# Seams of a two-layer transformer kernel: waits by bank, last value products, row copies and transposes are put elsewhere in the order

## The reference, cut to what matters

```
x = x + conv0(ln(x)); x = x + moe0(ln(x))     # layer 0
x = x + conv1(ln(x)); x = x + moe1(ln(x))     # layer 1
conv0: 12 heads of 32, all 1024 keys, relative position terms added to the scores,
       softmax, times values, output projection 384x384 with bias
conv1: 12 query heads, 4 key/value heads, a 7x7 window of keys, softmax, values, projection
moe  : logits = x @ Wr + b; the top 2 of 8 experts per token, softmax of the two;
       layer 0 routes only; layer 1 adds a shared expert of width 768
```

## Time and profile before

| What | Value |
|---|---|
| Median of three runs | 1117.99 us (1117.44 to 1119.78) |
| Profiled execution: time | 1120.67 us |
| Profiled execution: span of the instructions | 1119.1 us |
| PE busy | 1005.0 us, 90% of the span |
| DVE, ACT, POOL busy | 519.5, 322.8, 390.0 us |
| Mean granted clock of PE, share of full | 0.966 |

### The profile page before, as it was taken

How to read it: one execution, slowest core, us unless ns; L and a number is a source line. 1 busy time by engine, 2 the same in 40 slices (tenths; PEclk the granted TensorE clock), 3 DMA queues, 4 the chain that set the end, 5 groups by cost and what they waited for, 6 DMA issues and landing times.

```text
span 1119.1 us, 13486 instructions
## 1 busy us (share of the span) xinstructions
PE 1005.0 (90%) x4429; PEld 585.0 (52%) x4430; DVE 519.5 (46%) x910; ACT 322.8 (29%) x482; POOL 390.0 (35%) x333
## 2 busy tenths in 40 slices
PE   6999999999992499999588889899999999999998
PEld 3755555555441266665436655477444554455554
DVE  4555687788573055545446676671111111111114
ACT  3514545554621012222324545151111111111100
POOL 5514676677744201000533667353000000000004
PEclk9999999999996699999789999999999999999999
DMA  8699308000058235521326200613444434410005
GB/s 298 151 291 276 85 1 188 1 1 1 1 175 323 98 133 180 195 68 38 110 69 158 58 1 1 239 43 113 148 155 155 155 131 175 157 42 29 15 29 162
DMA packets 47177, 130.07 MB, mean 116 GB/s; under 512 B 7121, under 2 KB 26073, under 8 KB 46872
## 3 DMA queue, kind: packets, MB, share of 16 engines
q1 hardware_dynamic: 32360, 65.05, 19.7%
q0 software_dynamic: 14768, 64.37, 16.3%
HBM read 87.78 MB, written 30.61 MB: 106 GB/s over the span
## 4 chain that ended last, share of the span: by engine, by line
PE 72%; DVE 9%; issue 8%; DMA 4%; ACT 4%; POOL 1%; another core or an unknown queue 1%; SPq 0%; POOLq 0%; DVEq 0%; ACTq 0%
PE PS L1798 22%; PE PS L1819 11%; PE PS L1595 6%; PE PS L1513 5%; PE PS L1649 5%; PE PS L1771 4%; DMA Wd<-in_Wd_r 4%; DVE nmax_part L1239 3%; PE PS L1630 3%; PE PS L1735 3%; PE PS L1845 3%; PE PS L1632 2%; DVE exp_acc L1271 2%; PE PS L1573 2%; PE PS L1807 2%
## 5 line engine op out<-in xcount | busy, mean ns | idle before, releaser
L1798 PE MATMUL PS<-Wgu,xbT 128*128 x690 | 285.2, 555 | 9.2 <-DMA Wd<-in_Wd_r 5.5
L1798 PEld LDWEIGHTS PS<-Wgu,xbT 128*128 128x128 f32 x690 | 127.7, 191 | 127.3 <-issue 114.8
L1046 ACT ACTIVATE expS<-PS 128x1024 f32<-128x1024 f32 (+3 forms) x156 | 135.6, 878 | 119.2 <-PE PS L1632 117.6
L1819 PE MATMUL PS<-Wd,hidT 128*128 x414 | 143.0, 491 | 1.5 <-DVE hidT L1407 0.8
L843 POOL TENSOR_TENSOR exp_acc<-exp_acc,expS 128x512 f32<-128x512 f32 (+1 forms) x65 | 124.6, 1917 | 47.6 <-ACT expS L1046 46.8
L1239 DVE TENSOR_REDUCE nmax_part<-PS 128x1 f32<-128x512 f32 x160 | 103.7, 685 | 45.9 <-PE PS L1595 45.1
L1630 PE MATMUL PS<-QA,KS 128*128 128x512 f32 (+3 forms) x312 | 115.1, 375 | 9.8 <-ACT QB L1024 9.5
L1595 PE MATMUL PS<-KS,QA 128*128 128x512 f32 (+2 forms) x288 | 108.7, 423 | 13.2 <-DVE nmax L1239 5.2
L1632 PE MATMUL PS<-QB,KS 128*128 128x512 f32 (+3 forms) x312 | 110.7, 361 | 0.0
L1819 PEld LDWEIGHTS PS<-Wd,hidT 128*128 128x128 f32 x414 | 78.7, 191 | 57.7 <-issue 14.3
L947 POOL DMA_INDIRECT got<-block_rows_out,row_i x32 | 31.8, 993 | 209.1 <-DMA block_rows_out<-yb 199.9
(11 more groups left out here) (174 smaller groups left out, 1245.5 us busy)
## 6 DMA issues: line engine op xcount, KB each, us to landing
Wgu<-in_Wgu POOLq DMA_DIRECT2D x8, 1152.0 KB, 6.2
Wgu<-in_Wg_r POOLq DMA_DIRECT2D x8, 1152.0 KB, 6.2
Wgu<-in_Wu_r POOLq DMA_DIRECT2D x8, 1152.0 KB, 8.4
Wd<-in_Wd_r POOLq DMA_DIRECT2D x8, 1152.0 KB, 10.8
xb<-block_rows_in SPq DMA_DIRECT2D x46, 192.0 KB, 2.4
block_rows_out<-yb SPq DMA_DIRECT2D x46, 192.0 KB, 1.9
part_rows<-parts SPq DMA_DIRECT2D x2, 3072.0 KB, 17.4
Wd<-in_Wd POOLq DMA_DIRECT2D x8, 576.0 KB, 7.2
```

Source lines behind the costliest of these rows:

```text
L1046: act.activation(exp_tile(layer, c, unit)[:, pair, :].rearrange("p (b n) -> p b n", b=2)[:, :, lo:hi], PS[:, 2 * pair:2 * pair + 2, lo:hi] ...
L1798: last = pe.matmul(PS[:, 3 * par + lo // BANK, 0:n], xbT[:, par, kc, :], Wgu[layer][:, bass.ds(s, 1), kc, lo:lo + n], start=kc == 0, stop= ...
L1819: last = pe.matmul(PS[:, 7, 0:C], hidT[layer][:, par, i, :], Wd[layer][:, bass.ds(s, 1), i, :], start=i == 0, stop=i == m.IC - 1)
```

## The change: what it does

1. **Maxima wait by bank.** PE no longer waits for all jobs before the first piece. In layer 1 each of the first three pieces waits for the jobs in its own two banks; in layer 0, whose last jobs lie in banks 6 and 7, the pieces don't wait for jobs, and the first value product does.
2. **Last value products behind the rows.** In layer 0 one value product, in layer 1 two, move from between the pieces to behind `maxima_rows`; ACT copies them behind the first row copies.
3. **Row copies split within pairs.** In layer 1 ACT copied the rows of heads 0 and 1 and DVE those of 2 and 3. Now ACT copies 0 and 2, DVE 1 and 3, and ACT's second one stands behind the exponential of the unit's second pair.
4. **The last unit but one of layer 1** is no longer added up by POOL; PE sums it directly in `totals`, as it did already with the last.
5. **Transposes among projections.** The transposes of the first four tiles run before the last two projections, in both layers, and the first half's router product before the second half's transposes. ACT takes the second root after the copies of the first half.

Nothing that is computed changes, and no transfer is added.

The core of the diff:

```diff
-            if hb == 2 * BLOCKS - 1 and v == PER_HALF1 - 1:
+            if hb == 2 * BLOCKS - 1 and v >= PER_HALF1 - 2:
                 return []
...
+        VALUES_AHEAD = [NT - 1, NT - 2]
...
                 root(0)
-                if n % 2:
-                    root(1)
                 for kc in range(KC):
                     copy(0, kc)
-                if n % 2 == 0:
-                    root(1)
+                root(1)
                 copy(1, 0)
...
-                    if layer and pair:
-                        return
                     rows = 1 if layer == 0 else D
-                    for g in (2 * pair, 2 * pair + 1):
+                    for g in (2 * pair, 2 * pair + 1)[:2 - layer]:
...
-                for t in range(NT):
+                def copy_values(t):
...
+                for t in range(VALUES_AHEAD[layer]):
+                    copy_values(t)
...
                 copy_rows(0, 0, 0)
                 copy_rows(0, 0, 1)
+                for t in range(VALUES_AHEAD[layer], NT):
+                    copy_values(t)
...
-                    for g in range(2, G):
-                        last = dve.tensor_copy(QB[1][c % 2][D:2 * D, g, hb % HALF * BANK:(hb % HALF + 1) * BANK],
-                                               PS[D * g:D * g + D, 4, :])
-                    last.then_inc(nmax_dve, 1)
+                    for g in range(1, G, 2):
+                        dve.tensor_copy(QB[1][c % 2][D:2 * D, g, hb % HALF * BANK:(hb % HALF + 1) * BANK],
+                                        PS[D * g:D * g + D, 4, :]).then_inc(nmax_dve, 1)
...
-                for n in range(njobs - 8, njobs):
-                    evacuated(pe, layer, n)
...
+                    if t == 0:
+                        evacuated(pe, layer, 1 if layer else njobs - 1)
...
                     if hb % BLOCKS == 0:
+                        if layer and i < 3:
+                            evacuated(pe, layer, 2 * i + 3)
...
                     if u % (U[layer] // 2) == 0:
-                        if layer == 0:
-                            pe.wait_ge(nmax_act, 2 * (HALF * c + half) + pair + 1)
-                        elif pair == 0:
-                            pe.wait_ge(nmax_act, 2 * BLOCKS + HALF * c + half + 1)
-                        else:
-                            pe.wait_ge(nmax_dve, HALF * c + half + 1)
+                        pe.wait_ge(nmax_act, 2 * (BLOCKS * layer + HALF * c + half) + pair + 1)
+                        if layer:
+                            pe.wait_ge(nmax_dve, 2 * (HALF * c + half) + pair + 1)
...
-                    if end:
-                        lo, hi = units(layer)[U[layer] - 1][2:]
+                    for u in (range(U[layer] - 1 - layer, U[layer]) if end else ()):
+                        lo, hi = units(layer)[u][2:]
...
                     max_piece(first_block, i)
-                    if i % 2 == 1:
+                    if i % 2 == 1 and i // 2 < VALUES_AHEAD[layer]:
                         values(i // 2)
                 maxima_rows(first_block)
+                for t in range(VALUES_AHEAD[layer], NT):
+                    values(t)
...
                     last.then_inc(proj_psum, 1)
+                    if t == NT - 3:
+                        transposes(2 * layer + 1, 0)
...
-                transposes(2 * layer + 1)
+                router(layer, 0)
+                transposes(2 * layer + 1, 1)
+                router(layer, 1)
```

More of the change, by code:

```diff
@@ new lines, in transposes, with transposed @@
+            def transposes(n, half):
+                if n % 2:
+                    pe.wait_ge(proj_dve, NT * (n // 2) + 3 * (half + 1))
+                for kc in range(KC):
+                    for t in range(4 * half, 4 * half + 4):
+                        pe.wait_ge(xn_ready, NT * n + t + 1)
+                        last = pe.transpose(PS[:, 3 * half + kc, (t % 4) * P:(t % 4 + 1) * P], Xn[:, t, kc * P:(kc + 1) * P], ident[:, :])
+                    last.then_inc(xT_psum, 1)
+            def transposed(n, half):
+                pe.wait_ge(xT_act, 4 * n + 3 + half)
+                if half:
+                    pe.wait_ge(xT_dve, 2 * (n + 1))
@@ L1552, in _, with router @@
+            def router(layer, half):
+                transposed(2 * layer + 1, half)
+                pe.wait_ge(const_in, 16 * 4)
+                pe.wait_ge(proj_dve, NT * layer + 7 + half)
+                for kc in range(KC):
+                    last = pe.matmul(PS[0:E, 6 + half, :], router_w[:, layer, kc, :], XnT[:, kc, half * BANK:(half + 1) * BANK],
+                                     start=kc == 0, stop=kc == KC - 1)
+                last.then_inc(logits_psum, 1)
             for layer in range(2):
```

36 lines of the change are left out of this document (9 added, 27 removed).

## The result

The changed kernel takes 1107.1 us, the median of six runs (1104.3 to 1111.6), against 1117.6 us for the kernel before in the same six rounds (1112.1 to 1119.8): ratio 0.9923, 95% interval 0.9894 to 0.9952. A second set on another chip gave 1109.5 against 1116.6, ratio 0.9920 (0.989 to 0.995). By the two ratios 8.6 and 8.9 us are gone, about 8.8 (the medians of the first set are 10.5 apart); the forecast of 1110 had 8.0 us off the median shown before. One run of the experiments, of the kernel with part 3 alone, took 1499.53 us at a mean granted clock of 0.65 and counts in no ratio. The profiled execution of the changed kernel took 1107.34 us, with a span of 1105.8 us and a mean granted clock of 0.972. PE is busy for 1004.1 us of it, as before.

The account below looks back on a forecast made before the run. PE's waits at four seams, three idle stretches costing again by half clock, bound it. Terms 4.0 + 1.4 + 0.3 + 3.1 + 1.3 = 10.1; with clock parts halved, 8.2 off 1117.99: forecast 1110, range 1105.5 to 1114.

Parts of the forecast that it names:

- layer 0's seam: Start of layer 0's attention, PE's last job to the scores: 4.0 us gained, middle of 3.2 and 4.8.
- The steps on waits: At PE's seams: which wait ends last once the named one is gone, and the gain left by it.
- rival 3: Both layers' attention starts: transfers end last, taking away 1.7 + 1.35 and 1.1 us; 1114 us, chance 0.07.
- rival 1: Layer 0's router: its shortening counts there too, another 1.3 us; 1108.5 us, chance 0.08.
- rival 4: Layer 0's loop of 48 units: another rhythm, 0.33 us more wait per unit; 1125.8 us, chance 0.03.
- the price of half clock: Start of layer 0's attention: first two value-product passes 3.30 us, last 1.95, so 1.35 us lost.
- The start: Layer 0's attention: first value product starts at 65.4 instead of 67.12, 1.7 us gained.
- The clock parts: Gains from slowed stretches avoided in layer 0's attention start and layer 1's end: 1.35 + 0.8 + 1.7 = 3.9 us.
- a pair of terms: Layer 1's totals and projections, 3.1 us gained, and its router up to the shared expert, 1.3 us.
- two steps of part 4: Layer 1's totals: without clock 2.29 - 0.7 = 1.6, rounded to 1.4 us; clock gain counted half for the median.
- Rival 2: Whole kernel: clock gains are none, before lacking slowed stretches or the changed kernel getting its own; 1111.8 us, chance 0.20.
- six terms: Gains by seam: layer 0's attention 4.0; layer 1's 1.4, 0.3, 3.1 and 1.3; layer 0's router nothing.

Follow-up runs that it names:

- part 3 alone: Only the row copies split within pairs, on the kernel before: ratio 0.9990 (0.997 to 1.0011).
- parts 3, 4 and 5 alone: Three kernels, each the kernel before with just one of these parts: ratios 0.9990, 0.9971 and 0.9989.
- part 1 alone: Only the maxima's waits by bank, value products all still between the pieces, on the kernel before: 1114.62 us, ratio 0.9978.

## Why the prediction was right

Each seam without half clock and with it, in us, from the profiles named above:

| Seam | Without the part | With the part | Gain, like clock | Forecast |
|---|---|---|---|---|
| Layer 0: last job to first weighted product | 34.0, worked out below; 35.0 to 36.6 with half clock | 32.54; 34.2 with | 1.5 | 4.0, of it 1.8 without clock |
| Layer 1: last job to first scores | 13.09 | 11.48 | 1.6 | 1.4 |
| Layer 1: second to sixth rows | 68.79 | 68.61 | 0.2 | 0.3 |
| Layer 1: last rows to projections | 16.97; 17.2 to 18.3 with | 15.06 | 1.9 | 3.1, of it 1.4 without clock |
| Layer 1: projections to logits' transposes | 28.30 | 27.07 | 1.2 | 1.3 |
| Layer 0: projections to xb | 64.6 to 65.4 | 64.6 to 65.3 | 0 | 0 |

No profile of the old order is unfilled and at full clock over all of layer 0's seam. The 34.0 are 25.1 us to the rows (parts 3, 4 and 5 alone) and 8.9 from there on (part 1 alone). The kernel before with its idle time filled has 33.74: its first piece starts 0.10 us behind DVE's last low part instead of 0.35.

**The parts one by one.** By ratio parts 1 and 2 give 5.8 us, part 3 1.1, part 4 3.2 and part 5 1.2: 11.3 together, and 8.8 for all five. Each interval is about 2.2 us to either side, so the runs can't tell whether the parts add up. The seams say that part 3's 0.6 us is covered by part 2.

**The steps on waits held.** The waits that the forecast named are last: DVE's low part and not a transfer releases the value product (rival 3 falls), the reductions take the table load's place, PE itself is last in front of layer 1's scores, and in layer 0 POOL hides the router's gain (rival 1 falls). The loop of layer 0, from the first weighted product to the projections, takes 212.3 to 212.6 us in each of the fourteen profiles (rival 4 falls).

**The mis-sized term is layer 0's seam.** (The two rows that the forecast compared for the price of half clock, 3.30 and 1.95 us, are one value product of six passes each.) Its 4.0 us are exact for this pair of executions (36.55 to 32.54), because before had half clock in two places there and the changed one in none. Over the profiles, the five whose seam is as before and unfilled have a mean of 35.7 us (36.55, 36.55, 35.24, 35.21, 34.97), and the four with parts 1 and 2 and no filler one of 33.4 (32.54, 34.20, 34.19, 32.52): 2.3 us. The start was taken as 1.7 us from 67.12, but PE's two pieces ahead of the product already ran partly at half clock there: at full clock the product starts 2.9 us behind the last job, and 1.7 with the change, so 1.2. Part of the 2.3 us is exchanged with the time before: the two profiles with half clock at 66 us are the two that reached their last job 1.3 to 2.1 us sooner. Counted from the start of the span, the first projection of layer 0 comes at 313.1 us in the mean of the same five and at 311.3 in that of the four, 1.8 us sooner.

**The clock parts were halved for the median**, to 2.0 us. The sum of the table's gains at like clock is 6.4 us, beside the forecast's 6.2. With half of each clock part the forecast's terms are 2.9 at layer 0's seam, 1.4 and 0.3 in layer 1, and 3.5 from its last rows to the logits' transposes. The means over the profiles are 2.3, 1.6, 0.2 and 4.5 (46.6 us in the five profiles without parts 4 and 5, 42.1 with). That makes 8.6, beside 8.8 measured and 8.2 forecast. So a term that was 0.6 too large and a pair of terms that were 1.0 too small stand against each other, and that the sum came so near is in part luck. The second comes from two steps of part 4: its 1.6 us without the clock were rounded down to 1.4 and measure 1.9 (the added sums cost 0.6 us, 2.05 for 1.43 at full clock), and the slow stretch was there in five of six profiles, not in half of them.

**The clock of every run says much the same.** Each run's mean granted clock is on record. Of the 76 runs of the kernel before that stood beside the experiments, the 7 at 0.966 took 1120.2 us in the mean and the 24 at 0.972 took 1113.2; a straight line through all has 0.97 us for each 0.001. Their mean is 1116.2 us at 0.969. The changed kernel's twelve runs have a mean of 1108.4 at 0.972. By the line 2.8 of these 7.8 us are the clock's and 5.0 the order's. That is an estimate, since the line is that of the kernel before. The kernel before with its idle time filled has the changed kernel's clock and takes 1114.9, 6.5 us more. So at like clock the order is worth 5.0 to 6.5 us by these runs.

Rival 2 was half right: the changed kernel does get a half-clock stretch of its own, in two of four profiles, but not as often as before had its two, so 1111.8 was too high. The Trainium skill ("TensorE: Matmul & The Clock Gate", Part 1: the HAM clock gate) says that the monitor runs free of the kernel's start, so that the same kernel differs from run to run. Of the two pairs of profiles of the same instructions one agrees, the changed kernel's new seam, and the other doesn't show it: before's three seams came out alike twice. But both profiles of before also started alike: their first 18 job matmuls took 8.0 us, 9.6 to 11.0 in the twelve other profiles, and of the five profiles with that order and no filler these two alone have half clock at 66 us. At the new seam the two with 9.6 and 9.8 us have it and the two with 10.3 and 10.7 don't. So one profile's half clock at several seams isn't several independent draws. What speaks against the clock's share in this account is the kernel before with its idle time filled, which should have had 3 us and had 0.9 (up to 2.8); the share of the waits doesn't rest on it.

**Part 2** was valued at 0.1 and 0.3 to 0.4 us, and measures 0.3 and 0.5. The swap leaves PE's idle time about as long, and puts the product where half clock can hit it (3.83 us for 2.13).

## What to carry to other kernels

Where a wait is taken away, ask which wait ends last next, and take the gain from it; four of six terms came out within 0.2 us that way when clocks were alike, the other two within 0.5. Read a seam from two or more profiles before pricing it: half clock behind an idle stretch and a late engine come in some executions of the same instructions and not in others, and one execution shows only one of them. A load moved out of one transfer's way lands in the next one's: move it behind a landing, not behind an issue.

## What was not expected of the hardware

- Idle stretches of PE of about 2 us, between long busy stretches, are followed by half clock for 3 to 4 us in some executions and not in others. Ahead of the first piece of layer 0 (1.87 us idle): in two of five profiles. Behind the first rows of layer 0 (2.2 us): five of six. Ahead of the last totals of layer 1 (2.3 us): five of six. At the new place (1.98 us): two of four. Ahead of layer 1's first piece (1.8 us): none of five. Behind the first rows of layer 1 (1.73 us): one of five. Ahead of the first router product (2.25 us): three of seven in layer 0, one of seven in layer 1. Filled with matmuls: none of eight such places in four profiles, two of which had it seldom or never unfilled. At the totals and projections the same work took 1.6 us longer, at the moved product 1.7.
- ACT stood still for 7.0 and 10.0 us in one execution of fourteen, with its input ready and nothing that the profile names; it cost 5.2 us. What it waited for stays open.
- An xb read of 192 KB landed in 2.4 us with the DMA engines nearly free, and in 7.4 to 8.9 when a weight load of 2.3 MB had been issued 1.6 us before by another engine.
- The start of layer 1 varies by itself: from the first job's start to the last one's end 23.4 us in six profiles and 25.0 to 25.7 in eight, for the same instructions, as half clock reaches into it or not. What decides that was not tried.
